# Recurrence of a decoder layer: the key-value product is written back into PSUM, and the scan reads it there

## What is computed

```python
r = sigmoid(xr @ W_r.T); k = xk @ W_k.T; v = xv @ W_v.T
w = -softplus(-(xw @ W_w.T)) - 0.0001
def step(s, rkvw):                       # per batch and head, s is 8 x 8
    bonus = exp(u + k_t)[..., :, None] * v_t[..., None, :]
    o_t = einsum('bhi,bhij->bhj', r_t, s + bonus)
    s = exp(w_t)[..., None] * s + k_t[..., :, None] * v_t[..., None, :]
    return s, o_t
o = layernorm over the 8 channels of a head (o) * ln_w + ln_b
return (o * r) @ W_o.T
```

## Time and profile before

| | us |
|---|---|
| median of 3 runs | 1308.82 (1308.63 to 1311.33) |
| the profiled execution | 1307.34 |
| its span in the trace | 1305.6 |
| the stage's main loop, from the first spread to the end of the last scan | 43.65 to 122.37 |
| end of the stage's last VectorE instruction | 135.03 |

### The profile page before, as it was taken

One profiled execution on the slowest core, in us unless ns is written; L12 is line 12 of the kernel. 1 busy time (PEld: TensorE's weight loads), 2 busy tenths in 40 slices (PEclk: granted clock), 3 DMA queues, 4 the chain that ended last, 5 costly groups with the idle time before them and its releaser, 6 DMA issues. The chain is left out here.

```text
span 1305.6 us, 35729 instructions
## 1 busy us (share of the span) xinstructions
PE 1131.0 (87%) x14748; PEld 573.1 (44%) x14748; DVE 830.2 (64%) x1316; ACT 728.8 (56%) x1439; POOL 331.4 (25%) x664
## 2 busy tenths in 40 slices
PE   5988688988878999568999999999988885899997
PEld 2333334333323444235776766666765332322221
DVE  3998226887753332325776766776753635899994
ACT  4201343777753222545777666676654453599994
POOL 0644011333311333013422422422312433200000
PEclk8999767999998999779999999999998997899999
DMA  4000007111105320033012112100110003411100
GB/s 185 1 0 0 1 1 224 58 52 40 28 3 125 69 65 1 0 124 42 8 12 16 10 10 15 12 8 8 10 12 2 0 1 87 171 41 50 44 15 33
DMA packets 134479, 51.61 MB, mean 40 GB/s; under 512 B 103904, under 2 KB 126448, under 8 KB 133680
## 3 DMA queue, kind: packets, MB, share of 16 engines
q1 hardware_dynamic: 134284, 49.32, 15.8%
q10 hardware_dynamic: 36, 0.02, 0.0%
HBM read 33.12 MB, written 15.81 MB: 37 GB/s over the span
## 5 line engine op out<-in xcount | busy, mean ns | idle before, releaser
L1971 DVE TENSOR_REDUCE re_nmax<-ps 128x1 f32<-128x512 f32 x256 | 158.9, 683 | 89.4 <-PE ps L1739 89.3
L1882 ACT ACTIVATE re_p<-ps,re_nmax 128x512 f32<-128x512 f32 x256 | 158.9, 688 | 90.1 <-DVE re_nmax L1971 90.1
L1760 PE MATMUL ps<-const,re_p 128*128 128x128 f32 x1024 | 146.9, 283 | 7.4 <-ACT re_p L1882 4.8
L983 DVE TENSOR_REDUCE ga_nmax<-ps 128x2 f32<-128x1024 f32 x128 | 147.1, 1215 | 6.3 <-PE ps L747 6.3
L892 ACT ACTIVATE ga_pt<-ps 128x512 f32<-128x512 f32 x256 | 139.2, 598 | 16.7 <-PE ps L783 15.7
L1760 PEld LDWEIGHTS ps<-const,re_p 128*128 128x128 f32 x1024 | 110.3, 142 | 35.9 <-ACT re_p L1882 24.3
L983 DVE TENSOR_REDUCE da_nmax<-ps 128x2 f32<-128x256 f32 (+3 forms) x128 | 102.2, 820 | 33.6 <-PE ps L758 32.5
L892 ACT ACTIVATE da_pt<-ps 128x512 f32<-128x512 f32 (+3 forms) x256 | 96.9, 436 | 44.0 <-PE ps L783 41.8
L1888 ACT ACTIVATE re_pT<-ps 128x512 f32<-128x512 f32 x128 | 76.4, 597 | 28.7 <-PE ps L1760 20.9
L1254 DVE TENSOR_TENSOR ex_u<-ps,ex_s 128x512 f32<-128x512 f32 x48 | 33.2, 692 | 89.5 <-PE ps L1227 89.5
L1991 DVE COPY re_pT<-ps 128x512 f32<-128x512 f32 x128 | 82.3, 684 | 10.6 <-PE ps L1760 9.7
(11 more groups left out here) (390 smaller groups left out, 2015.6 us busy)
## 6 DMA issues: line engine op xcount, KB each, us to landing
ex_gates<-gates_scratch SPq DMA_DIRECT2D x4, 2048.0 KB, 14.1
da_qst<-da_stacks SPq DMA_DIRECT2D x32, 96.0 KB, 2.2
da_kst<-da_stacks SPq DMA_DIRECT2D x32, 96.0 KB, 2.3
ga_qst<-ga_stacks SPq DMA_DIRECT2D x32, 96.0 KB
ga_kst<-ga_stacks SPq DMA_DIRECT2D x32, 96.0 KB
da_stacks<-da_qkparts SPq DMA_DIRECT2D x6, 384.0 KB, 3.2
ga_stacks<-ga_qkparts SPq DMA_DIRECT2D x6, 384.0 KB, 2.9
weights<-in_weights SPq DMA_DIRECT2D x1, 2048.0 KB, 7.5
```

The costliest lines, as they stand in the source:

```text
L983: nc.vector.tensor_reduce(nmax[:, u % 2, :, pr, qt], g.ps[:, 2 * (step % S_GROUPS):2 * (step % S_GROUPS) + 2, 0:keys_of(qt)], AX.X, ALU.ma ...
L1760: last = nc.tensor.transpose(g.ps[:, bank_of("tile", s, idx), bass.ts(kt, 128)], p[:, QUAD_ORDER[idx], bass.ts(kt, 128)], g.c("ident"))
L1882: nc.scalar.activation(p[:, QUAD_ORDER[idx], :], g.ps[:, S_BANK + QUAD_ORDER[idx], :], ACT.Exp, bias=nmax[:, s % 2, idx:idx + 1]).then_inc ...
L1971: nc.vector.tensor_reduce(nmax[:, s % 2, idx:idx + 1], g.ps[:, S_BANK + quad, :], AX.X, ALU.max, negate=True).then_inc(maxed, 1)
```

## The change

The buffer `kv` in SBUF goes away. The multiply writes its product into the PSUM bank from which it read the spread values, and the scan reads its second input from there. The multiply no longer waits for `scanned`. A bank is in use until its scan has ended, so spread n waits for scan n-4 in place of multiply n-4.

```diff
-        kv, rs = sb("kv", [D, NB, T]), sb("rs", [D, NB, T])
+        rs = sb("rs", [D, NB, T])
@@ spread_values
                     if n < NB:
                         pe.wait_ge(evacuated, 5 * (B - 1) + (1, 3, 4, 5)[n])
                     else:
-                        pe.wait_ge(multiplied, n - NB + 1)
+                        pe.wait_ge(scanned, n - NB + 1)
@@ multiply
                     dve.wait_ge(vrepped, n + 1)
-                    if n >= NB:
-                        dve.wait_ge(scanned, n - NB + 1)
-                    nc.vector.tensor_tensor(kv[:, n % NB, :], g.ps[:, n % NB, :], k[:, n // HD, :], ALU.mult)\
+                    nc.vector.tensor_tensor(g.ps[:, n % NB, :], g.ps[:, n % NB, :], k[:, n // HD, :], ALU.mult)\
                         .then_inc(multiplied, 1)
@@ the scan
-                        nc.vector.tensor_tensor_scan(state[:, n % NB, 1:T + 1], a[:, b, :], kv[:, n % NB, :],
+                        nc.vector.tensor_tensor_scan(state[:, n % NB, 1:T + 1], a[:, b, :], g.ps[:, n % NB, :],
                                                      0.0, ALU.mult, ALU.add).then_inc(scanned, 1)
```

## The result

| | before | changed |
|---|---|---|
| median of 6 runs, us | 1308.72 (1305.34 to 1311.33) | 1296.62 (1291.07 to 1299.74) |
| span of the profiled execution, us | 1305.6 | 1289.3 |
| main loop, first spread to end of last scan | 43.65 to 122.37: 78.72 | 44.02 to 109.31: 65.29 |
| tail, to the end of the last VectorE instruction | 12.66 | 12.24 |

The ratio is 0.9906, with a 95% interval of 0.9879 to 0.9934: 12.3 us less, between 8.6 and 15.8. Medians give 12.1 us; 11.7 us were forecast, for a time of 1297.1. The two traces put 13.4 us into the loop and 0.4 into the tail. Their spans differ by 16.3 us. The loop starts 0.4 us later in the changed kernel's trace, and what is left, 1170.6 - 1167.8 = 2.8 us, lies behind the stage, where both kernels do the same.

The account below looks back on a forecast made before the run. VectorE was taken to bound the stage from 45 to 124 us. 13.3 - 0.7 - 0.9 = 11.7 us off the median 1308.82 gave 1297.1 us; own range 1295.0 to 1300.5, wider range 1294.5 to 1306.0.

Parts of the forecast that it names:

- point 1: Main loop: scans with one SBUF input no longer wait for GpSimd's product, 13.3 us saved over 32 scans.
- point 2: Main loop: reading the scan's second input from PSUM costs 0; the skill page's estimate was 65 ns a scan.
- point 3: Main loop: the multiply writing the PSUM bank it reads costs 0, upper end 532 ns each, 17.0 us in 32.
- A: Rival, main loop: the multiply pays for writing the bank it reads, 4.4 us slower, 1313.2 us; chance 0.11.
- B: Rival, main loop: PSUM access forbids instruction overlap, 0.15 us x 32 = 4.8 us, 1301.9 us; chance 0.14.
- point 5: Main loop: spread n's wait for scan n-4 is covered by two VectorE steps, with 1.2 us to spare.
- point 6: SBUF layout: kv leaves, later tensors move; nothing waits on GpSimd's product by more than 0.2 us.
- TensorE next in line: Main loop: TensorE's step equals VectorE's at 1.72 us, but its lead leaves some 3.5 us at the last spread.
- The clock: Main loop: TensorE's clock stays at 1.00, its two gate waits of 1.84 us becoming a few tenths.
- The tail: After the last scan: 12.66 us before, growing by 0.7 and 0.9 us to some 14 us.
- The gate's wait: Tail: the gate of batch 2 waits 1.26 us for its mean, and some 0.7 us more after the change.
- The 0.9 us for a pair at the lower clock: Tail: one more TensorE pair, output of batch 2 after a 1.5 us gate wait, runs slow, costing 0.9 us.

Follow-up runs that it names:

- e4: Changed kernel with the scan's second input an SBUF tensor again (projected values); ratio 1.0002 to the kernel before, loop 78.70 us.
- e5: Changed kernel with the multiply writing kv in SBUF again, the scan reading the spread values in PSUM; ratio 0.9913, loop 65.30 us.
- e10: Kernel before with GpSimd's product replaced by a memset of twice the columns, 0.95 us long; loop 64.51 us, scans 1210 ns.
- e1: Kernel before with only the wait changed: spread n waits for scan n-4 in place of multiply n-4; ratio 1.0003, loop 78.72 us.
- e6: Changed kernel with seven of eight sums L264 on TensorE cut to 64 of 512 columns; loop 65.28 us.
- e12: The changed kernel measured once more, beside the further version; 1291.93 us, ratio 0.9908 to the kernel before.
- e9: Changed kernel plus the token-mix difference and first gate instruction written to PSUM; 1294.08 us, ratio 0.9906 to the kernel before.

## Why the prediction was right

**The scan (point 1).** The step held: 13.3 us from rows 3 and 4 were forecast, and the scans' busy time fell by 13.3, the loop by 13.4. What was only argued then, that a scan with one SBUF input is free, e4, e5 and e10 now show. The Trainium skill, "SBUF — State Buffer", section "Who interferes with whom", says that two SBUF inputs on VectorE contend with a GpSimd instruction that reads SBUF, not with one that only writes it. The traces agree with both halves: 1622 ns beside the reading product (e4), 1210 ns beside the writing memset (e10). One reading of the rows was loose: the scan of rows 4, called started with GpSimd idle, began 0.07 us before the end of a product (52.41, 1.09 us long). It was not lengthened, since the product's end plus 1.08 us lies before its own 1.21. This scan is quite free, GpSimd's product having ended at 96.90 (rows 6):

```profile
97.25 1.21 DVE L410 TENSOR_TENSOR_SCAN rw_state<-rw_a,rw_kv 128x512 f32<-128x512 f32 x1
```

**The scan from PSUM (point 2).** Taken at 0. The shortest scans were 1.19 to 1.22 us with both inputs in SBUF, and the mean is 1.208 from PSUM. The next instruction still starts 1.13 us behind (60.89, then 62.02). The estimate of 65 ns from the Trainium skill's page "VectorE: DVE Perf Modes", section "The TRN2 errata", did not come out: the scans are 1208 ns from PSUM against 1210 from SBUF (e10), and 32 x 65 ns would be 2.1 us of loop.

**The multiply into PSUM (point 3).** Taken at 0, between 0 and 532 ns. It is 10 to 14 ns longer, and the scan starts 0.58 us behind it as before (60.31, then 60.89). Rivals A and B fall with that. (A's sum set 12.6 us against its 17.0, which is 13.3 less the 0.7 of the tail, without the 0.9 of the pair; by the forecast's own 11.7 us A would have stood at 1314.1 us, not 1313.2.) This was the widest of the unknowns and the reason that the range reached to 1306; one row of a VectorE write to PSUM would have taken the part above 1300.5 off it.

**The new wait (point 5).** e1 shows 0, as argued.

**`kv` out of SBUF (point 6).** It gives nothing (e4) and costs nothing (e5, which has it again, has the same loop). The sentence that nothing waits on GpSimd's product by more than 0.2 us was wrong, as rows 5 show a wait of 0.44 us on TensorE; it cost nothing, since VectorE is the bound.

**TensorE next in line.** Right that VectorE stays the bound (e6), though both steps are 1.72 us; the slack was mis-sized, 3.5 against 5.5 us. From the trace of the changed kernel: TensorE ended the last spread at 103.92, where the sum had it at 102.4, and VectorE began the multiply that needs it at 106.42, so 2.5 us lay there. The other 3.0 us are its waits before that, most of them in the early steps (65 pairs from 44.02 take 55.8 us at 0.43 us a pass, and the last spread began at 102.90, 3.1 us later); extra passes fill them, where I had counted 2 us as lost. The clock stayed at 1.00, as forecast: its waits for the two gates, 1.84 us before (rows 8), are 0.20 us and less:

```profile
81.73 1.13 PE L285 MATMUL ps<-rw_o,weights 128*128 128x512 f32 x2
...
98.50 1.12 PE L285 MATMUL ps<-rw_o,weights 128*128 128x512 f32 x2 [0.20 <-DVE rw_o L389]
```

**The tail, the step that was off.** It was to grow by 1.6 us and shrank by 0.4. These rows of the changed kernel answer rows 9:

```profile
107.00 2.31 DVE L408 TENSOR_TENSOR_SCAN rw_state<-rw_a,ps 128x512 f32<-128x512 f32 x2
111.30 0.75 DVE L386 SCALAR_TENSOR_TENSOR rw_o<-ps,vec,rw_sd 128x512 f32<-128x512 f32 x1 [1.99 <-ACT rw_sd L332]
...
120.86 0.69 DVE L394 TENSOR_TENSOR x<-ps,x 128x512 f32<-128x512 f32 x1 [1.22 <-PE ps L285]
```

The gate's wait grew from 1.26 to 1.99 us, by 0.73 where 0.7 was forecast. The 0.9 us for a pair at the lower clock did not come: TensorE waited 1.23 us for that gate, not 1.5, and the pair took 1.12 us, as pairs behind short waits do.

```profile
112.89 1.12 PE L285 MATMUL ps<-rw_o,weights 128*128 128x512 f32 x2 [1.23 <-DVE rw_o L389]
...
119.70 1.13 PE L285 MATMUL ps<-rw_o,weights 128*128 128x512 f32 x2 [3.01 <-DVE rw_o L389]
```

The last pair, too, ran at the full clock here, where the kernel before had 2.08 us behind the same wait, and that gave 0.95 us. It is not a gain of the change: in e12, the same kernel, this pair took 1.59 us, and in e9's trace VectorE again waited 2.17 us for it. Without that luck the tail is about 0.5 us longer than before (in e5, where this pair took 2.08 us, the tail is 13.18 us against 12.66). The sum also left out that the kernel before has a held product in its tail, the one of 1.92 us above, which pushes its last sums back. That may be why the tail without luck is longer by 0.5 us and not by the gate's 0.7; no run isolates it. With 13.4 us of loop less this 0.5, 11.7 becomes 12.9 us for the stage; the medians' 12.1 us can't tell the two apart.

## What to carry to other kernels

When an instruction's mean duration is above its shortest one, look in the timeline at what runs on the other engines at its start: here VectorE's two-input scans ended a fixed 1.08 us after GpSimd's instruction, however long that was. One engine had shut the other out, and the views count the time as busy, so no wait names it. If the second input is made from a PSUM bank anyway, leave it in PSUM: the write into the bank cost 10 to 14 ns. Then count the next engine's work per step before hoping for more; here it was equal, and only its lead kept it off the path.

## What I had not expected of the hardware

- GpSimd's writes don't hold a scan. A memset of 0.95 us beside a two-input scan left it at 1.21 us, and a scale of one tensor, shorter (0.62 us), stretched it to 1.27.
- VectorE reads and writes one PSUM bank in one instruction at its usual pace: 679 ns for 512 columns against 665, with the next instruction at the same distance.
- A scan that has started holds GpSimd's product in turn, by 0.8 us: 1.92 us in place of 1.09.
- The same pair of matmuls behind the same 3.0 us wait took 1.13 us (changed), 1.59 (e12) and 2.08 (before), and over all fourteen traces 1.12 to 2.08, so a single trace doesn't price a matmul behind a wait of this length.
